# Attention and expert layer on one core: one-pass turnings of the weights, another order at the start, and the tile pieces on GpSimd in other periods

## What is computed

```python
xn = layernorm(x)                                   # no gain, no offset
Q = einsum('bnd,hdk->bhnk', xn, proj_q)
K = einsum('bmd,dk->bmk', xn, proj_k); V = einsum('bmd,dv->bmv', xn, proj_v)
W = softmax(einsum('bhnk,bmk->bhnm', Q, K), axis=-1)
Y = einsum('bhnv,hdv->bnd', einsum('bhnm,bmv->bhnv', W, V), proj_o)
F = einsum('aemn,enh->amh', einsum('amh,ehn->aemn', xn, w1), w2)
out = x + Y + F
```

## Time and profile before

| | us |
|---|---|
| median of 3 runs | 1669.87 |
| lowest, highest | 1668.98, 1670.22 |
| the profiled execution's own time | 1669.67 |
| its span, first to last instruction | 1667.9 |

### The profile page before, as it was taken

The page is one execution under the profiler, slowest core; times in us unless marked ns, Lnnn a source line. Parts: engine busy times, 40 slices in busy tenths (PEclk is TensorE's granted clock), DMA queues, the critical chain, the costliest instruction groups (busy, mean ns, idle before and its releaser), DMA issues.

```text
span 1667.9 us, 46510 instructions
## 1 busy us (share of the span) xinstructions
PE 1634.7 (98%) x18820; PEld 1214.1 (73%) x18820; DVE 1239.3 (74%) x2655; ACT 1304.2 (78%) x1350; POOL 1379.9 (83%) x1008
## 2 busy tenths in 40 slices
PE   7999999999999999999999999999999999999998
PEld 6777777777777777777777777777777777777775
DVE  5777777777777777777777777777777777777775
ACT  4777877787787788778778777877878787787785
POOL 2788888888888888888888888888888888878876
PEclk9999999999999999999999999999999999999999
DMA  8000000000000000000000000000000000000000
GB/s 230 2 2 2 1 2 14 2 2 2 2 15 2 2 2 3 13 2 2 2 8 8 2 2 1 8 8 2 2 2 8 8 2 2 2 14 2 2 1 14
DMA packets 16769, 16.73 MB, mean 10 GB/s; under 512 B 432, under 2 KB 12976, under 8 KB 16560
## 3 DMA queue, kind: packets, MB, share of 16 engines
q1 hardware_dynamic: 15520, 13.24, 2.7%
q10 hardware_dynamic: 1040, 0.52, 0.1%
HBM read 9.57 MB, written 4.19 MB: 8 GB/s over the span
## 4 chain that ended last, share of the span: by engine, by line
POOL 56%; issue 24%; PE 18%; ACT 1%; DVE 0%; POOLq 0%; DMA 0%; SPq 0%; DVEq 0%; ACTq 0%
POOL pr_lo L306 40%; POOL xacc L318 9%; POOL xn L300 3%; PE s_ps L548 2%; PE s_ps L550 2%; PE s_ps L535 2%; PE t_ps L586 2%; PE t_ps L589 2%; PE t_ps L588 2%; POOL rstd L345 2%; POOL xacc L324 1%; POOL xn_lo L290 1%; PE s_ps L432 1%; PE s_ps L434 1%; PE s_ps L433 1%
## 5 line engine op out<-in xcount | busy, mean ns | idle before, releaser
L306 POOL TENSOR_TENSOR pr_lo<-pr,pr_hi 128x1024 f16<-128x1024 f32 x511 | 1086.4, 2134 | 264.3 <-ACT pr_hi L396 264.3
L389 ACT ACTIVATE pr<-s_ps,boost,scale 128x1024 f32<-128x1024 f32 x512 | 616.8, 1205 | 211.1 <-PE s_ps L550 210.3
L778 DVE TENSOR_REDUCE key_max<-s_ps 128x128 f16<-128x1024 f32 x512 | 624.0, 1219 | 0.0
L396 ACT ACTIVATE pr_hi<-pr 128x1024 f16<-128x1024 f32 x512 | 525.4, 1051 | 8.1
L548 PE MATMUL s_ps<-g_lo,xT 128*128 128x128 f16 x4096 | 512.4, 219 | 1.1 <-DVE g_lo L791 1.1
L550 PE MATMUL s_ps<-g_hi,xT 128*128 128x128 f16 x4096 | 512.3, 219 | 0.0
L548 PEld LDWEIGHTS s_ps<-g_lo,xT 128*128 128x128 f16 x4096 | 400.7, 98 | 31.6 <-DVE g_lo L791 1.6
L550 PEld LDWEIGHTS s_ps<-g_hi,xT 128*128 128x128 f16 x4096 | 400.8, 98 | 29.7
L586 PE MATMUL t_ps<-pr_hi,xn_hi 128*128 128x512 f16 x1024 | 388.7, 380 | 16.3 <-POOL pr_lo L306 14.4
L588 PE MATMUL t_ps<-pr_lo,xn_hi 128*128 128x512 f16 x1024 | 388.1, 379 | 0.0
L589 PE MATMUL t_ps<-pr_hi,xn_lo 128*128 128x512 f16 x1024 | 388.1, 379 | 0.0
(11 more groups left out here) (123 smaller groups left out, 1602.7 us busy)
## 6 DMA issues: line engine op xcount, KB each, us to landing
out_dram<-xacc SPq DMA_DIRECT2D x16, 256.0 KB, 2.3
w_sb<-in_L_ffn_w_dram SPq DMA_DIRECT2D x1, 2048.0 KB, 10.2
pr<-in_L_attn_proj_q_dram ACTq DMA_DIRECT2D x1, 512.0 KB, 4.7
xacc<-in_L_attn_x_dram SPq DMA_DIRECT2D x2, 256.0 KB, 5.1
pr<-in_L_attn_proj_o_dram SPq DMA_DIRECT2D x1, 512.0 KB, 6.5
xacc<-in_L_attn_x_dram SPq DMA_DIRECT2D x1, 384.0 KB, 11.0
xacc<-in_L_attn_x_dram SPq DMA_DIRECT2D x1, 128.0 KB, 6.3
wkv<-in_L_attn_proj_k_dram SPq DMA_DIRECT2D x1, 64.0 KB, 2.9
```

Of the source, the lines that this page charges most:

```text
L306: pool.tensor_tensor(pr_lo[:, u % RING, :], pr32[:, u % PR, :], pr_hi[:, u % RING, :], ALU.subtract)\
L389: act.activation(pr32[:, u % PR, :], both_banks(u), ACT.Exp, bias=boost[:, 0:1], scale=scale[:, 0:1])\
L396: act.activation(pr_hi[:, u % RING, :], pr32[:, u % PR, :], ACT.Copy).then_inc(p_hi_ready, 1)
L778: dve.tensor_reduce(key_max[:, u % 2, :], both_banks(u).rearrange("p (t q) -> p q t", q=P), AX_X, ALU.max).then_inc(keys_max, 1)
```

## The change

In the start, all the weights but wk and wv are turned by the transposing form of the product against the identity, in one pass. The subtraction of the first row is done elsewhere: for A by DVE on the turned wq (`wq_first`, and one subtraction in place of ACT's copy), for f by one product with `centre` in period 7. wo is turned behind the fold of A. The means on DVE come behind that subtraction, the statistics of tiles 8 and 9 behind A's scale. The low parts of the first four tiles move from DVE to POOL. ACT casts one head of A first, and the other seven behind block 0's g. Block 0 is projected right behind the first four tiles' turning; the second four tiles follow, in another bank. C is folded and emptied in two halves, the second inside period 0. All eight w1 are turned in periods 0 to 3, two a period, through one bank, emptied in turn by ACT and DVE; the eight folds stand in periods 4 and 5. The maximum of f is found in period 8 in place of 7.

In the loop, a tile's pieces on POOL and ACT move: root in period 0 of the next pair, normalising in period 1, ACT's cast in period 2, low part in period 3. Statistics and mean get two slots, used in turn (`ln_slot`).

The core of the diff:

```diff
             def normalise_next(tile):
-                pool.tensor_scalar(xn32[:, 0, 1:D], xacc[:, tile, 1:D], mean_var[:, AHEAD, 0:1],
-                                   rstd[:, AHEAD:AHEAD + 1], ALU.subtract, ALU.mult).then_inc(ln_xn32, 1)
+                slot = ln_slot(tile)
+                pool.tensor_scalar(xn32[:, 0, 1:D], xacc[:, tile, 1:D], mean_var[:, slot, 0:1],
+                                   rstd[:, slot:slot + 1], ALU.subtract, ALU.mult).then_inc(ln_xn32, 1)
...
-                if n % 8 == 2 and (tile := ln_tile(n // 8)) is not None:
-                    pool.wait_ge(ln_var, tile - AHEAD + len(FIRST_TILES) + 1)
...
-                if n % 8 == 3 and (tile := ln_tile(n // 8)) is not None:
-                    normalise_next(tile)
-                if n % 8 == 7 and (tile := ln_tile(n // 8)) is not None:
-                    xn_low(tile, 0, 1)
+                if (tile := ln_tile(n // 8 - 1)) is not None:
+                    if n % 8 == 0:
...
+                    if n % 8 == 1:
+                        normalise_next(tile)
+                    if n % 8 == 3:
+                        xn_low(tile, 0, 1)
...
-            act.wait_ge(transposed, 2)
-            act.activation(wqT, s_ps[:, 0:N].rearrange("p (h k) -> p h k", h=H), ACT.Copy).then_inc(evacuated, 1)
...
-            act.activation(a_hi[:, :, :], a_ps.rearrange("p (h k) -> p h k", h=H), ACT.Copy,
-                           scale=inv_scale[:, 0:1]).then_inc(hi_ready, 1)
-            for e in range(3):
-                empty_w1(e)
+            high_of_a(0, 1)
...
             g_high(0)
+            empty_c(0)
+            high_of_a(1, H - 1)
+            empty_c(1)
...
-                if n < 3:
-                    empty_w1(2 * n + 3)
+                if n < 4:
+                    empty_w1(2 * n)
...
-                if n % 8 == 6 and (tile := ln_tile(n // 8)) is not None:
+                if n % 8 == 2 and (tile := ln_tile(n // 8 - 1)) is not None:
                     split_high(tile, 0, 1)
...
-                last = pe.matmul(s_ps[:, h * P:(h + 1) * P], wq_sb[:, h, :], centre[:, :], start=True, stop=True)
+                last = pe.transpose(s_ps[:, h * P:(h + 1) * P], wq_sb[:, h, :], ident[:, :])
...
                 for c in range(MC):
-                    last = pe.matmul(w1_turn(e)[:, c * P:(c + 1) * P], w1_sb[:, e, c * P:(c + 1) * P], centre[:, :],
-                                     start=True, stop=True)
+                    last = pe.transpose(sum_bank(W1_BANK)[:, c * P:(c + 1) * P], w1_sb[:, e, c * P:(c + 1) * P], ident[:, :])
...
+                if n < 4 and rest:
+                    turn_w1(2 * n + place)
+                if n in FOLDS and rest:
+                    for e in range(2):
+                        fold_ffn(4 * FOLDS[n] + 2 * place + e)
...
+                if n == F_CENTRED:
+                    pe.wait_ge(f_copied, 1)
+                    pe.matmul(ffn_part(n), centre[:, :], f32w[:, :], start=True, stop=True).then_inc(f_ps, 1)
...
             spread_amax(0, None)
-            turn_w1(0)
-            turn_tiles(HT)
-            turn_w1(1)
             pe.wait_ge(weights_ready, 1)
             project(0)
-            turn_w1(2)
+            turn_tiles(HT)
+            fold_c(0)
...
+            dve.tensor_copy(wq_first[:, :], wq_turned[:, :, 0]).then_inc(wq_first_ready, 1)
+            dve.wait_ge(wq_first_ready, 1)
+            dve.tensor_tensor(wqT, wq_turned, wq_first[:, :].unsqueeze(2).to_broadcast([P, H, P]), ALU.subtract)\
+               .then_inc(evacuated, 1)
...
+                if n < 4:
+
+                    dve.wait_ge(w1_turned, 2 * n + 2)
+                    dve.tensor_copy(w1T[:, 2 * n + 1, :], sum_bank(W1_BANK)).then_inc(w1_evacuated, 1)
```

More of the change, by code:

```diff
@@ L169, in attention_ffn, with c_ps, first_turned @@
         a_ps = s_ps[:, 4 * BANK:6 * BANK]
-        def w1_turn(e):
-            return s_ps[:, (2 + e % 2) * BANK:(3 + e % 2) * BANK] if e < 3 else sum_bank(-2)
+        def c_ps(half):
+            return s_ps[:, (2 + half) * BANK:(3 + half) * BANK]
+        def first_turned(first):
+            return (t_ps[:, BANK:2 * BANK] if first == 0 else s_ps[:, 3 * BANK:4 * BANK]).bitcast(F16)
         def summing(n):
@@ L214, in turn_tile, with ln_slot @@
             return pair + NT if at == 0 and pair >= 1 and pair + NT < TILES else None
+        def ln_slot(tile):
+            return AHEAD + tile % 2
         def ln_tile(pair):
@@ L279, in _, with first_rstd @@
             pool.memset(centre[0:1, 0:1], 0.0).then_inc(consts, 1)
-            for g, (first, count) in enumerate(FIRST_TILES):
+            def first_rstd(g):
+                first, count = FIRST_TILES[g]
                 pool.wait_ge(ln_var, g + 1)
@@ L291, in xn_low @@
                                    xn_hi[:, at:at + tiles, 1:D], ALU.subtract).then_inc(xn_ready, tiles)
+            first_rstd(0)
+            first_rstd(1)
+            xn_low(0, 0, HT)
             xn_low(HT, HT, HT)
+            first_rstd(2)
             def normalise_next(tile):
@@ L453, in _, with fold_c @@
             last.then_inc(folded, 1)
[L454 to L458, removed]
+            pe.wait_ge(o_in, 16)
+            for h in range(H):
+                last = pe.transpose(s_ps[:, N + h * P:N + (h + 1) * P], wo_sb[:, h, :], ident[:, :])
+            last.then_inc(transposed, 1)
+            def fold_c(half):
+                pe.wait_ge(evacuated, 2)
+                if half == 1:
+                    pe.wait_ge(xT_ready, NT)
+                pe.matmul(c_ps(half), wkvT[:, P:2 * P], woT[:, half * BANK:(half + 1) * BANK], start=True, stop=True)\
+                  .then_inc(folded, 1)
             def turn_tiles(first):
@@ L462, in turn_tiles @@
                 if first:
-                    pe.wait_ge(xT_ready, first)
+                    pe.wait_ge(evacuated, 2)
                 for t in range(first, first + HT):
                     at = (t - first) * 2 * P
-                    pe.transpose(turn16[:, at:at + P], xn_hi[:, t, :], ident16[:, :])
-                    last = pe.transpose(turn16[:, at + P:at + 2 * P], xn_lo[:, t, :], ident16[:, :])
+                    pe.transpose(first_turned(first)[:, at:at + P], xn_hi[:, t, :], ident16[:, :])
+                    last = pe.transpose(first_turned(first)[:, at + P:at + 2 * P], xn_lo[:, t, :], ident16[:, :])
                 last.then_inc(xT_ps, 1)
@@ L727, in low_of_a @@
                 heads = a_ps.rearrange("p (h k) -> p h k", h=H)[:, first:first + count, :]
-                dve.wait_ge(hi_ready, 1)
+                dve.wait_ge(hi_ready, 1 if first == 0 else 2)
                 dve.scalar_tensor_tensor(out=a_lo[:, first:first + count, :], in0=heads, scalar=inv_scale[:, 0:1],
@@ L765, in _ @@
             power_of_two(0, None)
+            copy_first(0)
             low_of_a(0, 1)
-            for n in range(2):
-                dve.wait_ge(xT_ps, n + 1)
-                dve.tensor_copy(xT[:, :, n * BANK:(n + 1) * BANK].rearrange("p k (t c) -> p k t c", c=P),
-                                turn16.rearrange("p (t k c) -> p k t c", k=2, c=P)).then_inc(xT_ready, HT)
+            tile_stats(2)
+            tile_means(2)
+            copy_first(HT)
             def g_low(k):
```

112 lines of the change are left out of this document (66 added, 46 removed).

## The result

The changed kernel takes **1798.57 us** (median of 5 runs, 1796.39 to 1799.56) against 1669.42 us for the kernel before: a ratio of 1.0768, 95% interval 1.0754 to 1.0783. It is 129 us slower, inside the range and 67 us under the predicted 1866.

What follows compares the result with a forecast made beforehand. TensorE was taken to bound the steady part, with almost no room. From 1669.7 us, less 4 for the start, plus 131 for stalls and 69 for the clock, came 1866 us; range 1785 to 1905, holding 0.82.

Steps and rivals of the forecast that it cites:

- The chain of waits: Loop: ACT's cast waits for POOL's normalising, the exponential behind the cast, TensorE's product for the exponential; stall 2.70 us.
- the wait of the weighing: Loop: TensorE's wait for POOL's low halves, 0.27 us about once a pair, was to go.
- Stall less give-back: Loop, each of 54 tiles: 2.70 us stall less the 0.27 wait that goes, net 2.43 a pair, 131 us.
- The clock: TensorE's granted clock falls to half for 3.4 us behind most stalls: 69 us lost, bounds 0 and 92.
- The price of one fall: TensorE after a stall: each fall of the clock costs 1.6 us.
- four stalls in five: Loop: share of stalls taken to bring TensorE's clock down, 43 of 54.
- the rival that the clock holds, or few stalls bring it down: Loop: stalls come but TensorE stays at full speed, 1797 us; with cases near it 1785 to 1830, chance 0.20.
- The start: Before the loop's steady part: 4 us gained in all, bounds 0 and 7.
- Steps (1) to (3): Start up to the first key product: earlier fold, shorter order; product near 20.1, 4.8 us earlier, or 4 if clock falls.
- Step (4): Start, first key product to first weighing: 1.3 us less work, 2 us of waits, so 0.7 lost.
- the mechanism I had named: Start, periods 0 to 4: w1's turnings wait for their one bank's emptying, which on DVE precedes the bias; 2 us.

Runs made afterwards that it cites:

- run 1: Changed kernel with only the tile pieces put back in the periods of before, start still changed: 1669.85 us, ratio 1.0003.
- run 2: Kernel before with only the tile pieces, and the two slots they need, moved to the new periods: 1797.16 us, ratio 1.0765.
- run 3: Changed kernel with POOL's normalising ahead of the head's add in the same period, instead of behind it: 1750.01 us, ratio 1.0483.
- run 4: Changed kernel with the normalising one period earlier, right behind the root in POOL's idle time: 1644.76 us, ratio 0.9852.
- run 6: Changed kernel with three small unread copies on POOL ahead of each normalising, to lengthen the stall: 1872.99 us, ratio 1.1218.
- run 5: Kernel of run 2 with the normalising moved to the root's period, so the start of before with the loop of run 4: 1645.58 us, ratio 0.9855.
- run 7: Kernel of run 4 with a tiny activation put first on ACT to bring its table load forward: 1647.01 us, ratio 0.9867.
- run 8: Kernel of run 7 with 28 small unused products on TensorE between the spread of A's maximum and the projection: 1645.23 us, ratio 0.9858.

## Why the prediction was right, and where its terms were off

**The chain of waits was right**, place by place: ACT's idle time of 2.79 us (forecast 2.8), TensorE's stall at the ffn product of period u+4, 54 times, the wait of the weighing gone. Runs 1 to 4 tie the loss to the normalising's place: without the move no loss, the move alone the whole loss, 0.7 us out of the chain 0.7 us out of each stall, and the stall gone when the normalising is done in time.

**Stall less give-back, 2.43 forecast, 2.17 measured.** Two parts of this term were off, both the same way. The stall from start to start is 2.60, not 2.70: TensorE's next product was due at 818.93 + 0.22 = 819.15 and came at 821.75. ACT went from the cast to the exponential in 0.21 us (820.30 to 820.51), although the cast is listed as 0.31 long; I had added the whole 0.30. And the wait of before that comes back is 0.43 a pair, not the 0.27 of the earlier trace rows. These rows are of the kernel before:

```profile
812.92 0.22 PE L550 MATMUL s_ps<-g_hi,xT 128*128 128x128 f16 x1
813.41 0.39 PE L586 MATMUL t_ps<-pr_hi,xn_hi 128*128 128x512 f16 x1 [0.27 <-POOL pr_lo L306]
```

The 0.27 counts from the end of the last product, 0.22 after its start. But products in a row start every 0.056 us, so the next one was due at 812.98, and 0.43 us were lost. Run 4 shows it: without the wait, the pair is 0.44 shorter. 2.60 - 0.43 = 2.17. So the term is 117 us where I had 131, under its lower bound of 120, since the bounds were set on the stall (2.60 lies within its 2.5 to 2.9) and not on the give-back.

**The clock, 69 forecast, 12 measured.** This is the step that failed by most. The price of one fall was right (1.6 forecast, 1.7 measured); the count, four stalls in five, was not: 7 of 54 instead of 43. I had argued that an idle time of 1.8 us stands at the edge, from two places of the trace, and that one half as long again would mostly bring the clock down. By the lists of waits, stalls of 1.8 us (run 3) brought it down 0 times in 54, of 2.4 (the changed kernel, and run 2) 7 times, of 3.2 (run 6) 29 times. So the share rises with the length of the stall over these three lengths, and 1.8 us in the loop brought it down nowhere. The bounds for this term, 0 to 92, held it, and the rival that the clock holds, or few stalls bring it down, to which I gave 0.20 against 0.62 for the forecast, was the right case: the range held the time through that rival. It came out at 1797 against 1798.6 only because its start and its stalls were off the other way, by 10 us (-4 and +131 for 0 and 117), and hid the 12 us of clock that it left out.

**The start, 4 us gained forecast, less than 1 measured.** Steps (1) to (3) gave the first key product at 20.1, or 20.9 if the clock falls; it came at 22.73, 2.2 earlier than in the earlier trace rows and not 4. (Added up, 4 to 4.8 less 0.7 is 3.3 to 4.1; the sum took the upper end.) The rows of the changed start:

```profile
10.16 3.75 PE L476 MATMUL s_ps<-wkvT,pr 128*128 128x128 f32 x16 [1.61 <-DVE pr L808]
...
12.94 1.28 ACT L385 ACT_TABLE_LOAD   x1 [12.94 <-DVE xn L739]
14.23 1.14 ACT L385 ACTIVATE xn_hi<-xn 128x508 f16<-128x508 f32 x2
...
15.71 0.28 DVE L754 TENSOR_REDUCE amax_one<-s_ps 1x1 f32<-1x128 f32 x1 [0.47 <-PE s_ps L502]
...
16.76 0.38 PE L507 MATMUL s_ps<-amax_one,ones_row 1*128 1x1 f32 x2
...
18.81 0.61 PE L460 MATMUL t_ps<-xT,a_hi 128*128 128x512 f16 x1 [1.68 <-DVE a_lo L769]
...
22.73 1.06 PE L564 MATMUL s_ps<-g_hi,xT 128*128 128x128 f16 x8
...
25.10 0.60 PE L517 MATMUL t_ps<-ident,w_sb 128*128 128x128 f32 x4
```

The subtraction was done about when I said (the fold starts at 10.16, forecast 9.9), and the row of maxima started at 14.03 (forecast 13.8). What I missed is the table load. Now ACT's first activation is the cast that waits for DVE, and the load waits with it; before, it stood at 1.21, hidden, although the activation of its line waited for TensorE until 9.70:

```profile
1.21 1.28 ACT L368 ACT_TABLE_LOAD   x1 [1.21 <-PEq L923]
9.70 1.02 ACT L368 ACTIVATE pr<-s_ps 128x1024 f32<-128x1024 f32 x1 [7.21 <-PE s_ps L443]
```

By these rows some 0.7 us of its 1.28 lie on the path: the spread of the maximum stands behind the tiles' turning and starts at 16.76, though its number was there at 15.99 (15.71 + 0.28). The Trainium skill (ScalarE: Activation LUTs, What ACT_TABLE_LOAD costs) gives 1283 ns for a load, and the trace agrees. The projection then started at 18.81 (forecast 18.1), with the granted clock at 0.50 from 18.0 to 24.8, twice the 3.4 us of the earlier trace rows. That is one execution. In run 4's, where the clock was down for 3.4 us (19.7 to 23.1) as before, the same start has its first key product 3.35 us earlier than in the earlier trace rows:

```profile
21.57 1.06 PE L564 MATMUL s_ps<-g_hi,xT 128*128 128x128 f16 x8
```

So steps (1) to (3) gave 3.35 there, where I had 4 with a fall.

Step (4) was the larger miss. From the first key product to the exponential of unit 5 it took 25.97 us before and takes 29.89 now (22.73 to 52.62): 3.9 more, forecast 0.7. TensorE's busy time in it grew by 1.3 us (24.94 to 26.21) where I had 1.3 less, and its idle time by 2.65 where I had 2. Groups of that stretch in the changed kernel (busy us, mean ns | idle us before, releasers):

```profile
L577 PE MATMUL s_ps<-g_lo,xT 128*128 128x128 f16 x48 | 6.0, 219 | 0.9 <-DVE g_lo L844 0.9
...
L517 PE MATMUL t_ps<-ident,w_sb 128*128 128x128 f32 x32 | 5.1, 282 | 2.1 <-ACT w1T L390 1.3 <-DVE w1T L931 0.8
...
L601 PE MATMUL t_ps<-ident,minus_max 128*128 128x128 f16 x6 | 1.3, 220 | 0.7 <-DVE w1T L931 0.7
```

and of the turnings of w1 before, between its first key product and its unit 5:

```profile
L491 PE MATMUL t_ps<-centre,w_sb 128*128 128x128 f32 x40 | 5.7, 287 | 1.0 <-ACT w1T L365 0.9
```

The eight turnings have 5.1 us of busy time against 5.7 for the five of before: 0.6 saved where I had counted 2.2 (5.8 less 3.6), since a turning that is followed by a wait is listed to its end, with nothing beside it. Half of C's fold took 1.7 us, most of it at half clock, not 0.9, and the first key products 1.06 instead of 0.62. The waits are 2.1 us for the bank of the turnings and 1.6 for DVE's steps that stand behind the emptying of that bank: 3.7, against 1.0 before. That is the mechanism I had named, at 2.7 more instead of 2.

So in this execution 2.2 us are gained ahead of the key product and 3.9 lost behind it; in run 4's, 3.35 are gained and 3.5 lost (21.57 to 51.08 is 29.51). Over the runs the two starts come out alike (runs 1 and 5); in run 4, which has the changed start, unit 8's exponential begins at 62.07, and in the kernel before at 61.88.

The Trainium skill's rule on the transpose mode (TensorE: Matmul & The Clock Gate, Terms: four times faster for 32-bit data) isn't borne out here, against the 32-bit products with `centre`. The four products of a turning measure 0.44 us from their start to the next product's (25.10 to 25.54, the clock back at 1.00), near the 0.45 of the forecast: 0.11 for each pass, where the 1.16 of before had eight at 0.12. The number of passes halved, not their price; a quarter of 1.16 would have been 0.29.

## What to carry to other kernels

A step that waits on another engine, put ahead of work that is ready, makes that work wait for the whole chain behind the step; ask of each place in a queue what its input will have passed through by then, and use an idle stretch of the producer that ends before the consumer asks (here one period earlier turned +129 us into -24). Price a wait on a pipelined engine from start to start, against the spacing of its products, not by the idle time that the profile prints. A start rebuilt for one shorter path should be followed on every engine, down to the first instruction that each one now waits with.

## What the runs showed of the hardware

- Equal stalls brought TensorE's clock down in some places only. At 2.4 us it fell 7 times in 54, about once in eight pairs (222 us); at 3.2 us 29 times; at 1.8 us never in the loop, though one idle time of 1.77 us at the start did. So the length of a single idle time doesn't decide it alone.
- A DVE tensor_scalar of 128x127 took 1187 ns instead of 341 beside one GpSimd instruction of 1.15 us (run 7), and ended right behind it; beside another of 1.06 us, the root of four tiles, it kept its 340.
- A table load can stand behind the wait of its activation: it started at 12.94 in the changed kernel, and at 1.21 before, although that activation waited until 9.70. What decides between the two stays open; a tiny activation ahead moved it back to 1.21 (run 7).
- The fold of A took 3.75 us for sixteen products where it took 1.95 before, with a granted clock of 1.00 in the rows of both stretches. The ratio is that of half the clock, and TensorE had been idle 1.61 us ahead of it. The idle time alone doesn't do it: behind the same 1.61 us it took 3.38 in run 4, 3.67 in run 7 and 2.02 in run 8. What slowed it stays open.
